# Edge counting in a graph transformer: the order in which ScalarE empties PSUM at the borders between target tiles

## The chip, the cores and the metric

The kernel runs on one core of a Trainium2 chip. The metric is the time of one execution on the device in microseconds (us), lower being better. Three timed runs of the kernel before gave 2011.37, 2013.77 and 2014.79 us; the median is 2013.77 us. One more execution was recorded by the hardware profiler, and every row below is of that one.

## What is computed

Two layers of a graph transformer on 1250 nodes with 768 features and 20000 edges (`src`, `dst`, sorted by `dst`). In each layer a graph branch and a linear-attention branch are added to the residual stream, and a mixture of eight experts follows. The graph branch of the first layer is a graph attention with 12 heads of width 64; cut to what matters here:

```python
def gnn0(h, src, dst, W, attn_l, attn_r, W_res):
    ft = einsum('nhd,od->nho', h.reshape(n, 12, 64), W)
    a1 = sum(ft * attn_l, -1)
    a2 = sum(ft * attn_r, -1)
    e = leaky_relu(a1[src] + a2[dst], 0.2)
    w = exp(e - segment_max(e, dst)[dst])
    alpha = w / segment_sum(w, dst)[dst]
    agg = segment_sum(alpha[:, :, None] * ft[src], dst)
    return relu(agg + res)
```

The weight of an edge depends on its pair (src, dst) alone. So the kernel first counts how many edges each pair of nodes has, as a dense 1250 x 1250 matrix, and every sum over edges becomes a matmul with that matrix. The second layer's graph convolutions use the same counts.

## The kernel before

The nodes are cut into NT = 10 tiles of T = 125. The stage concerned is the **edge counting**, which lies between the projection of the first layer's linear attention and the attention over the graph; in the profile it spans some 374 to 537 us.

**The counts of one target tile.** For target tile g, VectorE walks over the tiles of 125 edges that can hold an edge to it, six slots (SLOTS) to a turn. For each edge tile it writes two one-hot matrices: OHD (125 edges x 125 targets, L1677) and OHS (125 edges x 1250 sources, L1679; three of its slots are called OHA and three OHB in the profile). TensorE multiplies them (L795) in three pieces of 418, 416 and 416 columns (CH) into three PSUM banks: banks 0 to 2 for even g, 3 to 5 for odd g. How many turns a target tile takes is read from the data (`table`, L788 on TensorE, L1666 on VectorE). In this input, target tile 0 takes 54 edge tiles, tile 1 takes 24, tiles 2, 3 and 4 take 18 each and tiles 5 to 9 take 12 each. VectorE may run six edge tiles ahead of TensorE (`oh_free`). A last tiny matmul of zeros (L806) signals `acc_done`.

**From counts to the matrix AT.** ScalarE copies the three banks into AROW (L1220, one of two buffers by g % 2): rows are targets, columns are sources. The attention wants it transposed. So TensorE turns the ten 125 x 125 blocks of AROW in three rounds `("at", g, q)` of 4, 4 and 2 transposes (L781), and ScalarE copies each round from PSUM into AT (L1205).

**Rounds for the features.** Two more rounds for each g, `("ft", g, 0)` and `("ft", g, 1)`, multiply the normalised features by the weights W (L775). ScalarE empties such a round with six copies into F, scaled by row factors (L1201).

**Two banks for all rounds.** All rounds share PSUM banks 6 and 7 in turn. The list TRR fixes one order for them, and TensorE, before it fills round r, waits until round r - 2 is emptied (`tr_emptied`, in `turn_round`). The order is

```python
    for g in range(NT + 1):
        if g < NT:
            TRR += [("ft", g, 0), ("ft", g, 1)]
        if g:
            TRR += [("at", g - 1, q) for q in range(3)]
```

**The order at a border.** For each g, TensorE issues the two ft rounds of g, then counts g, then signals `acc_done`, then issues the three at rounds of g - 1 (whose rows lie in AROW since the border before). The at rounds of the last tile follow behind the loop. ScalarE, written out by hand in the same way, empties the two ft rounds of g, waits for `acc_done` of g, copies the three pieces of the rows of g (L1220) and then empties the three at rounds of g - 1 (`empty_round`, L1193 to L1206). The rows of g are needed by TensorE only at the next border (`arow_ready`, L779), and their banks only when it begins to count g + 2 (L802). ScalarE works through its instructions in order; so does TensorE. No DMA and no GpSimd instruction takes part in a border. SyncE waits once for the last round (L513) before it loads the third block of rows for the attention.

Of the kernel before, what the change touches and what calls it, by code (L numbers as in the profile page):

```python
# [15 lines left out]
NT, T = 10, 125  # L16
# [124 lines left out]
def graph_transformer(nc, xn_d, y_d, x, src, dst, gW, gWT, gWresT, attnT, w0, wp0, bp0, rwT, rb, ewT, eb,  # L141
# [988 lines left out]
    def _(act):  # L1130
# [62 lines left out]
        def empty_round(r):  # L1193

            kind, g, q = TRR[r]
            act.wait_ge(tr_filled, r + 1)
            ps = PS[0:T, 6 + r % 2, :]
            if kind == "ft":
                for k in range(6):
                    h = 6 * q + k  # L1200
                    nc.scalar.activation(F[:, g, h, 0:D], ps[:, k * D:(k + 1) * D], ACT.Copy, scale=P2[:, g, h:h + 1])  # L1201
                nc.scalar.drain().then_inc(tr_emptied, 1)
            else:
                w = min(4 * q + 4, NT) - 4 * q
                nc.scalar.activation(AT[:, 4 * q:4 * q + w, g * T:(g + 1) * T],  # L1205
                                     ps[:, 0:w * T].rearrange("p (s n) -> p s n", s=w), ACT.Copy).then_inc(tr_emptied, 1)  # L1206

        round_of = {key: r for r, key in enumerate(TRR)}
# [4 lines left out]
        for g in range(NT):  # L1213
            for q in range(2):
                empty_round(round_of["ft", g, q])
            act.wait_ge(acc_done, g + 1)
            if g >= 2:
                act.wait_ge(tr_filled, round_of["at", g - 2, 2] + 1)
            for c, (o, n) in enumerate(CH):
                nc.scalar.activation(AROW[:, g % 2, o:o + n], PS[0:T, 3 * (g % 2) + c, 0:n], ACT.Copy).then_inc(arow_ready, 1)  # L1220
            if g >= 1:
                for q in range(3):
                    empty_round(round_of["at", g - 1, q])
        for q in range(3):
# [131 lines left out]
        for r in range(18):  # L1356
            q, c = r // 3, r % 3
# [22 lines left out]
        for r in range(18):  # L1380
            q, c = r // 3, r % 3
# [650 lines left out]
```

## Time and profile before

| | |
|---|---|
| median of three timed runs | 2013.77 us (2011.37 to 2014.79) |
| the profiled execution, its own time | 2016.99 us |
| its span (first to last instruction) | 2015.1 us |
| TensorE matmuls, busy | 1849.3 us, 92% of the span |
| VectorE busy | 746.1 us, 37% |
| ScalarE busy | 401.5 us, 20% |
| mean granted TensorE clock | 0.957 of full |

In the profile PE is TensorE's matmuls, PEld its loads of stationary operands, DVE VectorE, ACT ScalarE, POOL GpSimd, SP SyncE; L1220 is line 1220 of the kernel. Matmuls are pipelined, so their busy times overlap a little. "issue" in the chain of waits is time in which an engine waited for nothing that the profile shows. PEclk is the granted clock of TensorE as a share of full speed; the two levels are 2.4 GHz (1.00) and 1.2 GHz (0.50), and a stretch that holds both shows a value between.

### The profile page before, as it was taken

Reading aid. Unit: us, or ns where it says so; the run is one execution under the profiler, and the core shown is the slowest. Engines: PE = TensorE matmul, PEld = TensorE weight load, DVE = VectorE, ACT = ScalarE, POOL = GpSimd, SP = SyncE. Lnnn points to the kernel's source line nnn. Section 1 sums busy time; section 2 is a strip of 40 time slices with the busy share of each in tenths; the row PEclk is TensorE's granted clock in tenths of the full one; section 3 lists DMA queues with packets and bytes.
Section 4 is the critical chain, followed back from the end, with each engine's and each line's share of the span. In section 5 each row is a group of like instructions: output and inputs, shape, how many; then the busy total and the mean of one; then the engine's idle time right before and its main releaser. Section 6 shows DMA issues by size and latency. Waiting matters only on the chain.

```text
span 2015.1 us, 24539 instructions
## 1 busy us (share of the span) xinstructions
PE 1849.3 (92%) x8418; PEld 1165.9 (58%) x8419; DVE 746.1 (37%) x1688; ACT 401.5 (20%) x1065; POOL 128.5 (6%) x212
## 2 busy tenths in 40 slices
PE   7999999998899998599997999999999999599980
PEld 4555566566533344366666965555588589365650
DVE  3212222686688989511114311141111133311114
ACT  2431210024211222111102422000221211222110
POOL 0000000000000000111114100000000000111105
PEclk9999999999899999699998999999999999699995
DMA  6004000000000101545556111010010011545437
GB/s 183 0 1 165 3 1 0 20 1 1 14 35 33 44 28 42 196 142 185 190 185 169 55 47 47 0 47 0 1 47 1 0 55 47 203 141 182 177 117 229
DMA packets 58060, 153.06 MB, mean 76 GB/s; under 512 B 12526, under 2 KB 23170, under 8 KB 57525
## 3 DMA queue, kind: packets, MB, share of 16 engines
q1 hardware_dynamic: 34053, 87.05, 12.5%
q0 software_dynamic: 13120, 35.86, 5.9%
q10 hardware_dynamic: 10800, 28.98, 3.9%
q8 instruction: 56, 0.92, 0.2%
q14 instruction: 31, 0.25, 0.0%
HBM read 121.37 MB, written 33.99 MB: 77 GB/s over the span
## 4 chain that ended last, share of the span: by engine, by line
PE 81%; DVE 8%; DMA 5%; issue 2%; DVEq 2%; ACT 1%; POOL 1%; ACTq 0%; SPq 0%; POOLq 0%
PE PS L646 23%; PE PS L975 10%; PE PS L656 7%; PE PS L795 6%; PE PS L1016 4%; PE PS L1085 4%; PE PS L717 4%; PE PS L1105 4%; PE PS L1057 4%; DVE WRA L1727 3%; PE PS L1043 3%; PE PS L884 2%; DMA WS<-in_fW 2%; PE PS L893 2%; DVE WRB L1727 2%
## 5 line engine op out<-in xcount | busy, mean ns | idle before, releaser
L646 PE MATMUL PS<-WS,XT 128*125 128x384 f32 x960 | 313.3, 488 | 1.4 <-issue 1.4
L646 PEld LDWEIGHTS PS<-WS,XT 128*125 128x125 f32 x960 | 180.4, 189 | 129.3 <-issue 3.4
L975 PE MATMUL PS<-WS,XGT 128*128 x600 | 199.9, 491 | 0.0
L975 PEld LDWEIGHTS PS<-WS,XGT 128*128 128x128 f32 x600 | 113.2, 192 | 74.7 <-issue 2.5
L656 PE MATMUL PS<-XT,WS 128*128 128x416 f32 (+1 forms) x432 | 151.2, 512 | 0.0
L1727 DVE SCALAR_TENSOR_TENSOR WRA<-RB,U,AT 125x500 f32<-125x500 f32 (+1 forms) x240 | 140.1, 648 | 9.5 <-ACT AT L1205 6.8
L1856 DVE TENSOR_TENSOR YS<-PS,EBB 128x768 f32<-128x768 f32 x48 | 46.0, 958 | 256.9 <-PE PS L975 192.1
L656 PEld LDWEIGHTS PS<-XT,WS 128*128 128x128 f32 x432 | 81.6, 189 | 69.2 <-issue 69.2
L884 PE MATMUL PS<-WRA,F 125*64 125x500 f32 (+1 forms) x480 | 100.5, 537 | 10.1 <-DVE WRA L1727 9.5
L1085 PE MATMUL PS<-WS,XGT 128*128 x288 | 101.9, 505 | 7.6 <-DMA WS<-in_fW 4.9
L1105 PE MATMUL PS<-WS,HT 128*128 x276 | 94.5, 493 | 2.5 <-ACT HT L1414 2.5
L582 POOL DMA_INDIRECT XG<-xn_rows,IDX x52 | 50.9, 979 | 680.9 <-DVEq L1821 643.6
L1297 ACT ACTIVATE XGT<-PS 128x384 f32<-128x384 f32 x102 | 44.4, 489 | 223.0 <-DVE YS L1856 184.7
L1085 PEld LDWEIGHTS PS<-WS,XGT 128*128 128x128 f32 x288 | 54.9, 197 | 43.3 <-issue 13.4
L1016 PE MATMUL PS<-XT,WS 128*128 128x250 f32 x360 | 79.1, 381 | 0.6 <-issue 0.6
L646 PE MATMUL PS<-WS,QT 128*125 128x384 f32 x240 | 78.9, 486 | 0.0
L646 PE MATMUL PS<-WS,QK 128*125 128x384 f32 x240 | 77.6, 486 | 0.0
L1105 PEld LDWEIGHTS PS<-WS,HT 128*128 128x128 f32 x276 | 53.2, 193 | 39.8 <-issue 4.2
L717 PE MATMUL PS<-XT,WS 128*128 128x416 f32 (+1 forms) x216 | 76.1, 513 | 0.0
L1374 ACT ACTIVATE HF<-PS,DT 125x384 f32<-125x384 f32 x40 | 23.2, 580 | 262.8 <-PE PS L646 262.8
L1057 PE MATMUL PS<-HH,AT 125*125 125x384 f32 x400 | 73.8, 344 | 1.9 <-DVE HH L1939 1.9
L1016 PEld LDWEIGHTS PS<-XT,WS 128*128 128x128 f32 x360 | 69.3, 194 | 9.3 <-issue 1.0
(293 smaller groups left out, 2244.6 us busy)
## 6 DMA issues: line engine op xcount, KB each, us to landing
WS<-in_ewT SPq DMA_DIRECT2D x8, 2304.0 KB, 10.6
expert_rows<-YS ACTq DMA_DIRECT2D x48, 384.0 KB, 2.3
WS<-in_fW SPq DMA_DIRECT2D x16, 1152.0 KB, 7.5
WS<-in_w SPq DMA_DIRECT2D x5, 2304.0 KB, 10.4
xn_rows<-XN ACTq DMA_DIRECT2D x20, 336.0 KB
RB<-expert_rows SPq DMA_DIRECT2D x12, 488.3 KB
WS<-in_wp SPq DMA_DIRECT2D x2, 2304.0 KB, 11.5
WS<-in_W SPq DMA_DIRECT2D x2, 2304.0 KB, 8.1
```

The lines of the kernel that those rows point to most:

```text
L646: last = nc.tensor.matmul(ps[0:T, 0:HC], lhsT[:, k, t * T:(t + 1) * T], w[:, k, b * HC:(b + 1) * HC], start=(k == 0), stop=(k == KC - 1))
L656: last = nc.tensor.matmul(ps[:, 0:n], w[:, k, q * P:(q + 1) * P], rhs[:, k, o:o + n], start=(k == 0), stop=(k == KC - 1))
L717: last = nc.tensor.matmul(ps[:, 0:n], w[:, k, q * P:(q + 1) * P], XT[:, k, o:o + n], start=(k == 0), stop=(k == KC - 1))
L795: last = nc.tensor.matmul(PS[0:T, 3 * (g % 2) + c, 0:w], OHD[:, k, :], OHS[k][:, o:o + w], start=(first and k == 0), stop=True, skip_group ...
L884: last = nc.tensor.matmul(num[j * D:(j + 1) * D], F[:, s, 2 * p + j, 0:D], WR[k % WSLOTS][:, j, 0:n], start=(s == 0), stop=(s == NT - 1), ...
L975: last = nc.tensor.matmul(PS[:, 4 + 2 * a + b, 0:HC], XGT[:, a, k, :], WS[:, bass.ds(slot, 1), k * C + b * HC:k * C + (b + 1) * HC].rearra ...
L1016: last = nc.tensor.matmul(ps[:, 0:n], w[:, k, q * P:(q + 1) * P], XT[:, k, o:o + n], start=(k == 0), stop=(k == KC - 1))
L1043: last = nc.tensor.matmul(ps[:, 0:n], HH[:, v, s, q * P:(q + 1) * P], AT[:, s, o:o + n], start=(s + v == 0), stop=(s == NT - 1 and v == 1))
L1057: last = nc.tensor.matmul(ps[0:T, 0:HC], AT[:, s, t * T:(t + 1) * T], HH[:, v, s, b * HC:(b + 1) * HC], start=(s + v == 0), stop=(s == NT ...
L1085: last = nc.tensor.matmul(PS[:, 2 + a, 0:FH], XGT[:, a, k, :], WS[:, bass.ds(slot, 1), k * FH:(k + 1) * FH].rearrange("p a b -> p (a b)"), ...
L1105: last = nc.tensor.matmul(PS[:, 5 + b, 0:HC], HT[:, k, :], WS[:, bass.ds(slot, 1), o:o + HC].rearrange("p a b -> p (a b)"), start=(k == 0) ...
L1727: V.scalar_tensor_tensor(out=WR[k % WSLOTS][:, j, 0:nt * T], in0=RBS[u % RSLOTS][:, j, 0:nt * T], scalar=U[:, s, h:h + 1], in1=AT[:, s, t0 ...
```

## The change

For g from 1 to 8, ScalarE empties the three at rounds of tile g - 1 before it waits for `acc_done` of g and copies the rows of g. For g = 9 the order stays as it was, and for g = 0 there are no at rounds. TensorE's, VectorE's and all other instructions are the same, and ScalarE issues the same instructions as before, in another order.

```diff
         for g in range(NT):
             for q in range(2):
                 empty_round(round_of["ft", g, q])
+            if 1 <= g < NT - 1:
+                for q in range(3):
+                    empty_round(round_of["at", g - 1, q])
             act.wait_ge(acc_done, g + 1)
             if g >= 2:
                 act.wait_ge(tr_filled, round_of["at", g - 2, 2] + 1)
             for c, (o, n) in enumerate(CH):
                 nc.scalar.activation(AROW[:, g % 2, o:o + n], PS[0:T, 3 * (g % 2) + c, 0:n], ACT.Copy).then_inc(arow_ready, 1)
-            if g >= 1:
+            if g == NT - 1:
                 for q in range(3):
                     empty_round(round_of["at", g - 1, q])
         for q in range(3):
             empty_round(round_of["at", NT - 1, q])
```

## Rows read from the trace of the kernel before

**Rows 1.** The page: busy time of TensorE; its granted clock in 40 slices.

```profile
PE 1849.3 (92%) x8418; PEld 1165.9 (58%) x8419; DVE 746.1 (37%) x1688; ACT 401.5 (20%) x1065; POOL 128.5 (6%) x212
...
PEclk9999999999899999699998999999999999699995
```

**Rows 2.** Chain of waits, 374 to 545 us: by line; the border at 441 us (start, length).

```profile
by line: PE PS L795 64.9%; PE PS L775 12.1%; ACT AROW L1220 7.0%; ACT AT L1205 5.0%; issue 3.9%; PE PS L884 3.6%; PE PS L781 3.3%; DVE WRA L1727 0.8%; PE PS L806 0.3%
...
440.99 0.05 PE PS L806
...
441.06 1.34 ACT AROW L1220 x3
442.40 0.49 ACT AT L1205
...
442.94 0.49 PE PS L781 x2
443.45 0.39 ACT AT L1205
...
444.26 2.13 PE PS L775 x12
446.39 10.73 PE PS L795 x54
```

**Rows 3.** Waits, 374 to 545 us (total us, times, longest).

```profile
PE PS L781 <- ACT AT L1205: 8.9, 10, 1.0
PE PS L775 <- ACT AT L1205: 6.6, 8, 0.8
...
DVE OHD L1677 <- PE PS L795: 34.3, 20, 3.8
```

**Rows 4.** Chain of waits, the last border, at 533 us.

```profile
534.66 1.19 PE PS L781 x6
...
535.88 0.60 ACT AT L1205
...
536.51 0.49 PE PS L781 x2
```

**Rows 5.** TensorE's timeline (start, length; idle before): transposes at 441, two pauses elsewhere.

```profile
440.86 1.11 PE L781 MATMUL PS<-ident,AROW 125*125 125x125 f32 x8
...
1479.38 3.87 PE L1043 MATMUL PS<-AT,HH 125*128 125x418 f32 x19 [1.91 <-ACT HH L1376]
...
1628.99 4.26 PE L1057 MATMUL PS<-HH,AT 125*125 125x384 f32 x14 [1.87 <-DVE HH L1939]
```

**Rows 6.** Chain of waits: the border at 410 us, which has no transposes.

```profile
409.77 0.79 issue
410.56 1.57 PE PS L775 x12
```

**Rows 7.** Chain of waits: behind the border at 457 us.

```profile
460.36 1.57 PE PS L775 x12
461.93 9.63 PE PS L795 x54
```

**Rows 8.** Windows (start:end length, busy time of each engine, PEclk, DMA share, GB/s).

```profile
444.20:448.00 3.80, 3.73 (x18) 3.16 (x19) 0.46 (x3) 2.67 (x12) 0.00 (x0) 0.62 0.00 0
...
460.30:464.00 3.70, 3.64 (x25) 3.14 (x26) 1.60 (x6) 2.58 (x12) 0.00 (x0) 1.00 0.00 0
...
1479.40:1483.00 3.60, 3.60 (x19) 3.55 (x20) 0.00 (x0) 0.00 (x0) 0.00 (x0) 1.00 1.01 393
...
1629.00:1632.50 3.50, 3.50 (x12) 3.50 (x13) 0.00 (x0) 0.00 (x0) 0.00 (x0) 0.58 1.02 376
```

**Rows 9.** VectorE's timeline: the first six one-hot pairs of target tile 6.

```profile
495.36 0.26 DVE L1677 TENSOR_SCALAR OHD<-iota,ES 125x125 bf16<-125x125 f16 x1 [1.51 <-PE PS L795]
...
498.60 0.55 DVE L1679 TENSOR_SCALAR OHB<-iota,ES 125x1250 bf16<-125x1250 f16 x1
```

**Rows 10.** Chain of waits: TensorE's counting of target tile 6.

```profile
501.10 7.48 PE PS L795 x36
```

## The prediction, made before the changed kernel ran

> **What bounds the kernel now.** The page comes first: TensorE is busy for 92% of the span, so little can be won but where it waits, or where its clock is below full [rows 1]. The clock row says that full speed is not held throughout, which matters below. Then the chain of waits over the counting stage. Most of it is TensorE's: counting (L795), the feature rounds (L775), the transposes (L781). But 7.0% are ScalarE's row copies (L1220) and 5.0% its copies into AT (L1205) [rows 2]. They are on the chain at each border with transposes, and the border at 441 us shows how. Counting ends at 440.99; ScalarE copies the three pieces of rows for 1.34 us; only then does it empty the first transposed round (0.49), which sets free the bank for TensorE's last two transposes at 442.94. The copy of the second round shares that stretch, the third follows (0.39), and the next feature rounds begin at 444.26. The rows just copied are wanted by nobody until the next border.
>
> The waits give the total: TensorE waits 8.9 us in ten waits for the copies into AT before transposes, and 6.6 us in eight before feature rounds. VectorE waits 34.3 us for TensorE, so it isn't the bound here [rows 3].
>
> **The change, part by part.**
>
> *Row copies off the chain.* The change concerns eight borders (g = 1 to 8). ScalarE issues the same 3 + 3 copies; nothing is added or removed, on no queue. The 3 row copies (1.34 us) leave the path at each, but not all of that is won, because the first transposed round must be filled before it can be emptied. TensorE starts the first eight transposes at 440.86 [rows 5]. What follows if ScalarE stands ready is seen in the last border, where the rounds of tile 9 meet an idle ScalarE: six transposes take 1.19, of which the first two take 0.49 as in rows 2, so four take 0.70. Then 0.03 until the copy, 0.60 for the copy (0.49 when another stands just before it), 0.04 until the next transposes: 0.70 + 0.03 + 0.60 + 0.04 = 1.37 us from the first transpose of a round to the round that reuses its bank [rows 4]. At 441 us the same distance is 442.94 - 440.86 = 2.08 [rows 2, 5]. **Gain 0.71 us a border, 8 x 0.71 = 5.7 us.** Bounds: 0 if the next wait takes it all, 1.34 x 8 = 10.7 if the fill cost nothing. I take the measured distance.
>
> *Do the feature rounds follow?* They start 444.26 - 442.94 = 1.32 after the last two transposes. Two things lie in it: ScalarE's third copy, and TensorE's own reading of the table for the next tile. The border at 410 us has no transposes at all, and there TensorE still pauses 0.79 us, all "issue" [rows 6]. Behind the last transposes (442.94 + 0.49 = 443.43) the pause is 0.83, nearly the same. So the table reading sets it, it starts behind the transposes, and moves with them. The copies: first emptied at 440.86 + 1.33 = 442.19, second 442.68, third fill at 442.23 + 0.49, emptied by 443.14. The feature rounds at 442.94 - 0.71 + 1.32 = 443.55 wait for neither.
>
> *The row copies in their new place.* They run from 443.14 to 444.48. Behind them on ScalarE queue the feature copies (L1201), whose first round is only filled some 0.9 us behind 443.55; so they lose nothing, and nobody needs them before the next border. Cost zero, under cover of TensorE's feature rounds and counting (over 7 us at the shortest). The next tile counts into the banks of tile g - 1, copied a border earlier.
>
> *VectorE as the next one late.* Behind a border TensorE needs edge tiles. Six were made in 495.36 to 499.15, 3.79 us, or 0.63 each [rows 9]; TensorE takes 9.63 / 18 = 0.535 each at full clock [rows 7]. VectorE is slower by the piece, but the border gives it time: here its sixth piece is ready at 499.15, and TensorE begins to count at 501.10 [rows 10]. With both savings of this border (0.71, and 0.60 that half clock adds to the feature rounds there) it would begin near 499.8 and reach the sixth 5 x 0.535 = 2.7 us later. Cost zero. For target tile 0 VectorE does set the pace, but that is before the change acts.
>
> *The clock.* Behind the border at 441 us the granted clock is 0.62, behind the one at 457 it is 1.00 [rows 8]. Feature rounds and 18 edge tiles take 2.13 + 10.73 = 12.86 us in the first case and 1.57 + 9.63 = 11.20 in the second [rows 2, 7]: a fall to 1.2 GHz costs 1.66 us. In the windows and the chain, five of the eight borders concerned show such a fall (428, 444, 475, 499, 523 us), three don't (460, 488, 512), although the pauses are alike. In each TensorE idles in two parts: between the first eight transposes and the last two (442.94 less 440.86 + 1.11, or 0.97 [rows 2, 5]) and ahead of the feature rounds (0.83), 1.8 us; the change takes 0.71 of the first and leaves 1.1 us. What did the clock do elsewhere? Behind 1.91 idle us at 1479 it stayed at 1.00, behind 1.87 at 1629 it fell [rows 5, 8]; behind 0.79 at 410 it stayed, since the feature rounds took 1.57 as at full clock [rows 6, 7]. So 1.8 us is where it can go either way, and 1.1 us lies towards the shorter pause, where it held. **Gain: 5 x 1.66 = 8.3 us if all falls go.** Bounds: 0, or a loss of 3 x 1.66 = 5.0 if all eight borders fall.
>
> The Trainium skill ("TensorE: Matmul & The Clock Gate", "A second HAM failure mode: psum-queue depth-cycling") holds that many brief idle moments between groups of matmuls suffice for the clock to swing up and down. By that rule the falls would stay, and this term would be 0 instead of 8.3 us. The trace bears it out only as far as the pauses of 1.8 us go.
>
> *Sum.* 5.7 + 8.3 = 14.0 us from the profiled execution's own 2016.99 gives 2003.0. That execution's span is 2015.1, with 1.9 around it, and its time lies 3.2 us over the median. If the 3.2 is what profiling adds, the median becomes 1999.8. If it is that the timed runs had two falls fewer (2 x 1.66 = 3.3), they have fewer to win, and the median becomes 2003. I can't tell which, and take **2002**.
>
> **The rivals.**
>
> *The falls stay.* If pauses of 1.1 us serve the fall as well as 1.8, only 5.7 us are won: 2008.1 on the median, 2011.3 on the profiled time. For it speaks that the fall is not governed by the idle time alone (like pauses, unlike outcomes). Against it: the 410 us border, and the attention stage behind this one, which is full of small waits, with the clock near full in its slices [rows 1]. With some falls left it lies between 2002 and 2008.
>
> *No gain: the next wait takes it.* The feature rounds stay where they are because they wait for something that doesn't move. Against it: each candidate (third copy, table reading, VectorE) starts from an event that does move. The change does what it says, since the wait for `acc_done` is what stands ahead of the copies now. Time: 2013.8.
>
> *Slower: more falls.* TensorE's clock falls at each of the eight borders and again in the counting behind it, 16 stretches in place of 5: 11 x 1.66 = 18.3 lost, 5.7 won, 12.6 us slower, 2026. It decides from 11 falls on the counting stage: (11 - 5) x 1.66 = 10.0 less 5.7 is 4.3 us slower. For it: the moment of a fall depends on more than the pause. Against it: no border shows two falls, and the change takes idle time away and puts none in.
>
> **How the numbers follow.** Falls gone 0.66 (2002); falls stay in part or whole 0.21 (2005 to 2011); no gain 0.10; slower 0.03. A measurement of this kernel tells 0.2%, about 4 us, from no change. Faster by more than that: all of the first, most of the second (5.7 us is just over the bound): 0.84. Within it: 0.13. Slower: 0.03. Range: 1998 (both gains off the median, and near 2 us that three runs scatter) to 2009 (only the first gain, on the median).
>
> **What would show it.** In the changed kernel's profile: at eight borders the copy into AT starts some 0.7 us behind the first transposes, the last two transposes 1.37 behind it, and the row copies stand behind the third AT copy; the wait of TensorE's transposes for ScalarE falls from 8.9 to about 3 us, that of the feature rounds stays near 0.8 each under whatever name. Counting behind 18-tile borders takes 9.63 each time, with PEclk at 1.00 in all. The last border is unchanged. The stages from 537 us on have their old lengths, but start some 14 us sooner. Wrong it would be if feature rounds still began 3.3 us behind the end of counting, if PEclk below 1.00 stood behind borders with shorter pauses, or if a later stage grew by as much.

## The result, and the profile after

The changed kernel takes 1999.29 us (median of four runs, 1998.45 to 1999.94) against 2012.57 us before (four runs, 2009.52 to 2014.79). The ratio is 0.9931 with an interval of 0.9919 to 0.9944, which is 11 to 16 us less. The forecast was 2002, with 1998 to 2009 as its range.

The profiled execution (1999.16 us, span 1997.3) shows the borders in another form. First the chain of waits in the changed kernel from 374 to 545 us: its shares by line, then the border at 440 us (start, length, what), to be held against [rows 2].

```profile
by line: PE PS L795 62.6%; PE PS L775 9.6%; PE PS L884 8.2%; PE PS L781 5.9%; ACT AT L1205 5.5%; issue 3.8%; PE PS L893 2.7%; DVE WRA L1730 0.8%; ACT AROW L1223 0.8%; DVEq L1667 0.5%; PE PS L806 0.1%
...
440.02 0.01 PE PS L806
440.03 0.55 PE PS L781 x4
440.58 0.02 issue
440.60 0.60 ACT AT L1205
441.20 0.04 issue
441.24 0.49 PE PS L781 x2
441.74 0.02 issue
441.76 0.39 ACT AT L1205
442.15 0.42 issue
442.57 1.57 PE PS L775 x12
444.14 9.63 PE PS L795 x54
```

The row copies (now L1223) fell from 7.0% of the chain to 0.8%, which is the last border, left as it was. In their place stand the first four transposes and the first copy into AT. From the end of counting to the feature rounds it was 444.26 - 440.99 = 3.27 us, and is 442.57 - 440.02 = 2.55. Over the eight borders these stretches sum to 26.0 us before and 20.2 after: **5.8 us from the order**. The feature rounds with the counting behind them take 1.57 + 9.63 here, where the same border had 2.13 + 10.73.

ScalarE's timeline of the changed kernel at the same border shows where the row copies went (start, length, instruction, idle before).

```profile
440.60 1.54 ACT L1205 ACTIVATE AT<-PS 125x500 fp32r<-125x500 f32 x3 [8.06 <-PE PS L781]
442.04 1.33 ACT L1223 ACTIVATE AROW<-PS 125x418 f32<-125x418 f32 x3
443.52 2.77 ACT L1201 ACTIVATE F<-PS,P 125x64 f32<-125x64 f32 x12
```

Three AT copies, three row copies, and the feature copies start 0.95 us behind the feature rounds' own start at 442.57, as early as they could before: the row copies are fully covered.

Windows on the changed kernel, from each of two of the eight feature rounds on (start:end length, busy time of each engine, PEclk, DMA share, GB/s); the other six read 1.00 too.

```profile
442.50:446.20 3.70, 3.63 (x25) 3.13 (x26) 2.15 (x8) 3.45 (x15) 0.00 (x0) 1.00 0.00 0
...
501.50:505.00 3.50, 3.47 (x24) 3.02 (x25) 2.02 (x7) 3.29 (x15) 0.00 (x0) 1.00 0.00 0
```

**All five falls of the clock are gone**: 1.57 + 4 x 1.66 = 8.2 us. The waits of the changed kernel from 374 to 545 us (total, times, longest):

```profile
DVE OHD L1680 <- PE PS L795: 21.2, 17, 1.6
...
PE PS L775 <- ACT AT L1205: 6.5, 8, 0.8
...
PE PS L781 <- ACT AT L1205: 3.1, 10, 1.0
```

Against [rows 3], TensorE's wait ahead of transposes fell from 8.9 to 3.1 us, that ahead of the feature rounds stayed (6.6 to 6.5), and VectorE waits 21.2 us in place of 34.3. The whole stage, from the feature rounds of tile 0 to the first attention weight of VectorE, went from 163.33 to 149.05 us, 14.3 less: 5.8 from the order, 8.2 from the clock at these borders, and 0.3 from the counting of target tile 0 (35.64 to 35.37 us with its feature rounds), which the change does not touch.

The two profiled spans differ by 17.8 us. The stage began 1.6 us later in the changed kernel and gave 14.3. The other 5.1 us are 0.9 between the stage and the first gather of tokens, 1.5 from there to the last store of expert rows, and 2.7 behind it. No instruction differs there. From the end of the stage to the end of the span it was 1477.7 and 1474.3 us in two profiles of the kernel before (the second is below) and 1472.5 and 1476.2 in two of the changed kernel. The two ranges overlap, so these 5 us are scatter between executions and are not credited to the change. Of the 0.9 us, 0.8 can be located: the first 16 matmuls of the attention (L884), at half clock in their first part, took 6.10 us before and 5.27 in the changed kernel.

### The profile page after: what moved, and what is told of

Same layout as the page of the kernel before. It is cut to its first block, busy times and chain, and to the rows that moved or that the text cites. A ratio compares the mean times of both kernels' runs of the same rounds, so it can differ in the third digit from the quotient of the medians.

```text
span 1997.3 us, 24539 instructions
## 1 busy us (share of the span) xinstructions
PE 1838.2 (92%) x8418; PEld 1157.3 (58%) x8419; DVE 745.1 (37%) x1688; ACT 401.4 (20%) x1065; POOL 128.5 (6%) x212
## 4 chain that ended last, share of the span: by engine, by line
PE 81%; DVE 8%; DMA 5%; issue 2%; DVEq 2%; ACT 1%; POOL 1%; ACTq 0%; SPq 0%; POOLq 0%
PE PS L646 23%; PE PS L975 10%; PE PS L656 8%; PE PS L795 5%; PE PS L1016 4%; PE PS L1085 4%; PE PS L717 4%; PE PS L1105 4%; PE PS L1057 4%; DVE WRA L1730 4%; PE PS L1043 3%; PE PS L884 2%; DMA WS<-in_fW 2%; PE PS L893 2%; DVE WRB L1730 2%
## 5 line engine op out<-in xcount | busy, mean ns | idle before, releaser
L884 PE MATMUL PS<-WRA,F 125*64 125x500 f32 (+1 forms) x480 | 100.1, 535 | 10.1 <-DVE WRA L1730 9.5
```

The lines of the kernel that those rows point to most:

```text
L884: last = nc.tensor.matmul(num[j * D:(j + 1) * D], F[:, s, 2 * p + j, 0:D], WR[k % WSLOTS][:, j, 0:n], start=(s == 0), stop=(s == NT - 1), ...
```

## The experiments

Two numbers describe the borders of a kernel. **Idle** is TensorE's idle time there: its waits for ScalarE ahead of the transposes (less the 1.2 us of the last border) and ahead of the feature rounds, over eight. **Falls** are the borders of g = 1 to 8 whose feature rounds and counting take 1.6 to 1.7 us longer than at full clock. The stage is measured as above, in the profiled execution; idle, falls and stage are thus of one execution each. A ratio compares a kernel with runs of the kernel before on the same chip, so kernels are compared with each other by their ratios rather than by their medians.

| kernel | idle, us | falls | stage, us | time, us | ratio to before (interval) |
|---|---|---|---|---|---|
| before | 1.8 | 5 | 163.3 | 2012.57 | |
| before, again | 1.8 | 4 | 161.5 | 2012.87 (one run) | |
| changed | 1.05 | 0 | 149.1 | 1999.29 | 0.9931 (0.9919 to 0.9944) |
| changed, again | 1.1 | 0 | 149.2 | 2000.23 | 0.9926 (0.9912 to 0.9940) |
| old order, idle time filled | 0.8 | 0 | 155.0 | 2004.46 | 0.9951 (0.9938 to 0.9965) |
| new order, two copies ahead | 1.9 | 5 | 164.4 | 2016.71 | 1.0013 (1.0004 to 1.0022) |
| new order, one copy ahead | 1.5 | 2 | 156.2 | 2007.03 | 0.9967 (0.9956 to 0.9979) |
| first round only | 1.45 | 0 | 152.4 | 2004.18 | 0.9954 (0.9940 to 0.9967) |
| borders 1 to 4 only | 1.05 / 1.8 | 1 | 153.9 | 2005.47 | 0.9967 (0.9955 to 0.9980) |
| new order at all nine borders | 1.05 | 0 | 150.2 | 2002.4 | 0.9949 (0.9932 to 0.9967) |
| old order, table read early | 0.95 | 0 | 147.9 | 1999.14 | 0.9926 (0.9910 to 0.9942) |
| new order, table read early | 0.25 | 0 | 142.1 | 1993.33 | 0.9900 (0.9885 to 0.9915) |

**The kernel before, again.** No edit.

> The kernel before, profiled once more, to see how many of its borders fall to half clock in another execution. Theory A (a fall costs 1.66 us and sits behind borders with 1.8 us of idle time): counting stage 374 to 537 us again near 163 us, 2 to 6 of the eight borders with a feature round and count stretch 1.66 us longer, the others at full clock. Theory B (the falls of the first trace were an accident of that execution): none or one, and the stage near 155 us.

Four borders fell (429, 474, 498 and 511 us), the other four did not, and the stage took 161.5 us. So falls are a trait of the kernel before, at changing borders, and not of one execution.

**The clock alone: the idle time filled in the old order.** The fillers write into banks that the next tile's counting clears anyway.

```diff
                 for q in range(3):
+                    if q == 2 and g < NT - 1:
+                        for _ in range(2):
+                            nc.tensor.matmul(PS[0:T, 3 * ((g + 1) % 2), 0:2 * P], XT[:, 0, 0:T], WBD, start=True, stop=True)
                     turn_round(round_of["at", g - 1, q])
```

> The old order of ScalarE, with two matmuls of 256 columns whose result nobody reads put into TensorE's idle 0.97 us ahead of the last two transposes of borders 1 to 8. It isolates the clock. Theory A (the clock falls because TensorE idles there): distances at a border unchanged (2.08 us to the last transposes, 3.3 us to the feature rounds), no falls, 5 x 1.66 = 8 us faster, near 2004. Theory B (falls don't depend on this pause): 2 to 6 falls stay, 2012 as before. Theory C (the fillers delay the transposes): up to 8 x 0.5 = 4 us of the gain is eaten.

TensorE's timeline of this kernel at one border:

```profile
439.63 1.12 PE L781 MATMUL PS<-ident,AROW 125*125 125x125 f32 x8
440.59 1.03 PE L812 MATMUL PS<-WBD,XT 128*125 128x256 f32 x4
441.71 0.48 PE L781 MATMUL PS<-ident,AROW 125*125 125x125 f32 x2
443.00 1.57 PE L775 MATMUL PS<-WBD,XT 128*125 128x128 f32 x12 [0.81 <-ACT AT L1208]
```

The last two transposes start 2.08 us behind the first, as before. Over the eight borders the stretches from the end of counting to the feature rounds sum to 26.1 us against 26.0, so nothing was won by order. Yet no border falls, the stage is 8.3 us shorter, and the ratio says 7 to 12 us. Work that nobody reads makes the kernel faster because TensorE keeps its clock. Theory A holds.

**The pause put back in the new order.** In the changed kernel, ahead of the first AT copy:

```diff
             if 1 <= g < NT - 1:
+                act.wait_ge(tr_filled, round_of["at", g - 1, 0] + 1)
+                for i in range(2):
+                    nc.scalar.activation(AROW[:, g % 2, 416 * i:416 * i + 416], X[:, g, 0:416], ACT.Copy)
                 for q in range(3):
                     empty_round(round_of["at", g - 1, q])
+                nc.scalar.drain()
```

> The new order, with two copies of 416 columns from SBUF to AROW (which the row copies overwrite later) ahead of the first AT copy at borders 1 to 8: the pause is put back without the row copies. Distance from first transposes to the last two goes from 1.36 to about 2.2 us. Theory A: the order term comes back as 8 x 0.85 = 6.8 us and the falls come back too, 4 to 5 x 1.66 = 7 to 8 us, so 2013 to 2014, as the kernel before. If the clock does not depend on the pause but on something else that the new order changed: 6.8 us only, near 2006.

TensorE's timeline at a border that fell:

```profile
426.12 1.11 PE L781 MATMUL PS<-ident,AROW 125*125 125x125 f32 x8
428.36 0.48 PE L781 MATMUL PS<-ident,AROW 125*125 125x125 f32 x2 [1.12 <-ACT AT L1205]
429.66 1.91 PE L775 MATMUL PS<-WBD,XT 128*125 128x128 f32 x12 [0.82 <-ACT AT L1205]
```

The distance is 2.24 us, the stage 164.4, five borders fall, and the time is as before, even 0.1% over it. The new order alone is worth nothing where the pause stays. That it is a little slower fits the pause, 0.16 us longer at each border than in the kernel before.

**Half the pause.** The same with one copy (`range(1)`).

> The new order with one copy of 416 columns instead of two ahead of the first AT copy: TensorE idles some 1.1 + 0.5 = 1.6 us a border. The order term of 8 x 0.5 = 4 us comes back. Falls between none (as with 1.45 us where only the first round was moved) and 4 or 5 (as with 1.8 us): 2003.5 if none, 2011 if five.

TensorE idles 0.68 us ahead of the last two transposes and 0.82 ahead of the feature rounds. Two borders fell in the profile and the stage took 156.2 us. The median of 2007.03 lies between the two cases; 12 runs spread from 1999.01 to 2010.44, the widest of all kernels here.

**Only the first round in the new order.** Against the changed kernel:

```diff
             if 1 <= g < NT - 1:
-                for q in range(3):
+                for q in range(1):
                     empty_round(round_of["at", g - 1, q])
...
-            if g == NT - 1:
-                for q in range(3):
+            if g >= 1:
+                for q in range(0 if g == NT - 1 else 1, 3):
                     empty_round(round_of["at", g - 1, q])
```

> New order for the first transposed round alone at borders 1 to 8: ScalarE empties round 0, then copies the rows, then empties rounds 1 and 2. The last two transposes start as early as in the changed kernel (1.36 us). Theory A: now the feature rounds wait for round 1 to be emptied, 0.55 + 0.02 + 0.60 + 1.34 + 0.49 + 0.04 = 3.0 us behind the end of counting, against 3.27 before and 2.54 in the changed kernel: 8 x 0.23 = 1.8 us from the order; TensorE idles some 1.45 us a border, so falls may stay or go (0 to 5 x 1.66): 2002.5 to 2011. Rival (only the table reading behind the transposes sets the feature rounds): they start at 2.54, all falls gone, 1999 as the changed kernel.

TensorE's timeline at a border:

```profile
440.51 1.11 PE L781 MATMUL PS<-ident,AROW 125*125 125x125 f32 x8
441.86 0.48 PE L781 MATMUL PS<-ident,AROW 125*125 125x125 f32 x2 [0.24 <-ACT AT L1205]
443.57 1.58 PE L775 MATMUL PS<-WBD,XT 128*125 128x128 f32 x12 [1.23 <-ACT AT L1205]
```

The last two transposes start 1.35 us behind the first, but the feature rounds wait 1.23 us, for the copy of round 1 behind the row copies. From the end of counting they start at 443.57 - 440.64 = 2.93 us (3.0 expected, 2.54 by the rival). Here a ScalarE copy sets them; in the changed kernel it does not. No border falls. That also tells something on the length of single pauses: the longest here, 1.23 us, is longer than any at a border of the kernel before (0.97), where about half of the borders fell. So the longest single pause does not decide, and the sum of the pauses (1.45 us here, 1.8 there) puts these kernels in the right order.

**Four borders.** The conditions of the change read `1 <= g < 5` and `g >= 5`.

> The new order at borders 1 to 4 alone; 5 to 8 as before. Theory A (each border stands by itself): 4 x 0.72 = 2.9 us from the order, no falls at borders 1 to 4, two or three at 5 to 8, so 2.9 + 2.5 x 1.66 = 7 us of the changed kernel's 14: near 2006.5. Rival (falls move to the borders that keep their pause, all four of them fall): 2.9 + 1 x 1.66 = 4.6 us, near 2009.

Borders 1 to 4 pass without a fall. Of borders 5 to 8, which keep the long pause, one fell (503 us). So the falls don't gather on the borders that keep their pause, and 2005.47 is close to the 2006.5 of theory A; on the same chip the changed kernel took 2000.23.

**The last border too.** The new order at g = 9 as well.

> The new order at the last border too (g = 9), which the change leaves out. There the rows are needed at once by the rounds of tile 9. In the changed kernel 520.04 to 524.75 = 4.7 us pass from the end of counting to the last AT copy; with the new order 2.1 us for the rounds of tile 8, then 1.34 for the rows, then 0.70 + 0.03 + 0.60 + 0.04 + 0.49 + 0.02 + 0.39 = 2.3: 5.7 us, so 1.0 us slower than the changed kernel, 2000.3. Rival (the new order is as good there): 1999 or less.

The chain of waits of this kernel at the last border:

```profile
519.60 0.01 PE PS L806
519.61 0.55 PE PS L781 x4
...
521.62 1.34 ACT AROW L1223 x3
522.96 0.14 issue
523.10 0.68 PE PS L781 x4
...
524.96 0.39 ACT AT L1205
```

From the end of counting to the last copy it is 525.35 - 519.60 = 5.75 us against 4.71 in the changed kernel. Here the fresh rows are what is waited for, and the old order is right. The stage is 1.1 us longer. The 3 us between the medians (2002.4 and 1999.29) are not evidence: the two kernels were not timed side by side, and the intervals of their ratios overlap.

**The table read early.** TensorE reads its two table entries for g + 1 behind the first turn of counting g.

```diff
+        def entries(g):
+            return (nc.tensor.value_load(table[0:1, 1, g:g + 1], min_val=2, max_val=TURNS),
+                    nc.tensor.value_load(table[0:1, 2, g:g + 1], min_val=0, max_val=TURNS * NT))
+
+        ahead = entries(0)
         for g in range(NT):
-            n = nc.tensor.value_load(table[0:1, 1, g:g + 1], min_val=2, max_val=TURNS)
-            done_before = nc.tensor.value_load(table[0:1, 2, g:g + 1], min_val=0, max_val=TURNS * NT)
+            n, done_before = ahead
...
             counted(done_before, True)
+            if g + 1 < NT:
+                ahead = entries(g + 1)
```

> The new order, and TensorE reads the table entries of tile g + 1 behind the first turn of counting tile g instead of at the border. Theory A (the table reading is what sets the feature rounds, and it moves): the pause ahead of the feature rounds goes from 0.83 us to next to nothing, and they start when round 1 is emptied, 0.55 + 0.02 + 0.60 + 0.49 + 0.04 = 1.70 us behind the end of counting instead of 2.54: 8 x 0.84 = 6.7 us, and 0.79 at the border behind tile 0, 7.5 in all; near 1992. Rival (the third AT copy sets them): 2.11 + 0.04 = 2.15, 3 us only, near 1996. Rival (reading stalls TensorE's queue in the counting instead): 1999, as the changed kernel.

The chain of waits of this kernel, one border:

```profile
438.69 0.01 PE PS L812
438.70 0.55 PE PS L781 x4
439.25 0.02 issue
439.27 0.60 ACT AT L1211
439.87 0.04 issue
```

TensorE's timeline behind it:

```profile
439.91 0.48 PE L781 MATMUL PS<-ident,AROW 125*125 125x125 f32 x2 [0.24 <-ACT AT L1211]
440.39 0.81 PE L775 MATMUL PS<-WBD,XT 128*125 128x128 f32 x5
```

The feature rounds follow the last transposes at once, 440.39 - 438.70 = 1.7 us behind the end of counting, as theory A had it. The stage loses 6.9 us against the changed kernel. Of the 7.5 expected, 0.4 went to VectorE at target tile 1: TensorE now arrives sooner there, feature rounds with 24 edge tiles take 1.41 + 13.38 us in place of 1.57 + 12.84, and from 411 to 425 us VectorE is busy for 14.00 of 14.00 us (13.74 in the changed kernel). At **1993.33 us (ratio 0.9900, 0.9885 to 0.9915) this is the fastest kernel of the study**, ahead of both. The same early reading in the old order of ScalarE:

> The old order of ScalarE, and only the early reading of the table. Theory A: the last two transposes still start 2.08 us behind the first, the feature rounds follow when round 1 is emptied, 0.07 + 1.34 + 0.49 + 0.49 + 0.04 = 2.4 to 2.6 us behind the end of counting in place of 3.27: 8 x 0.7 = 5.6 us and 0.8 at the first border. TensorE's idle time per border drops to about 1.0 us, so the falls go too (5 x 1.66 = 8.3): near 1999, as the changed kernel. If only ScalarE's order matters for the falls: 6.4 us, near 2007.

The feature rounds start 2.43 us behind the end of counting, no border falls, and 1999.14 us equals the changed kernel (ratios 0.9926 and 0.9931) without touching ScalarE. It is another way to the same shorter pause.

**The changed kernel, again.** No edit.

> The changed kernel once more, beside the kernel before on another chip. Theory A (the executions of the kernel before scatter because the number of falls at its borders differs, and the changed kernel has none): near 1999.3, its runs within some 2 to 3 us of each other, those of the kernel before over some 8 us. If the falls are only moved or rarer: its runs scatter as widely as those of the kernel before.

The time came out (2000.23), the scatter did not: five runs from 1994.92 to 2002.22, while ten of the kernel before lay between 2010.78 and 2015.02. Its profile has no fall and a stage of 149.2 us. So the falls at these borders are not the main source of scatter between executions. TensorE's clock in other stages is a candidate. In these five runs the mean granted clock was 0.966, 0.965, 0.963, 0.962 and 0.962 for 1994.92, 1996.82, 2000.23, 2000.84 and 2002.22 us, and the 12 runs with half the pause go from 0.966 for the fastest to 0.959 to 0.960 for the four slowest. One place is in the traces: the first 16 matmuls of the attention took 5.27 us in one profile of the changed kernel and 6.46 in the other, against 3.50 for 16 of them at full clock. How much of the scatter that makes up stays open.

## Why the prediction was right

- **Row copies off the chain.** Forecast 8 x 0.71 = 5.7 us, measured 5.8. The 1.37 us taken from the last border came out as 1.35, since a fill and a copy by an idle ScalarE are the same pieces there.
- **The feature rounds follow.** Forecast 1.32 us behind the last transposes, as before; measured 442.57 - 441.24 = 1.33. The early reading of the table shows by experiment that TensorE's own reading filled that pause: moved away, the feature rounds start where the transposes end.
- **The row copies in their new place.** Forecast zero, measured zero at these borders. The first-round-only kernel shows what they cost where the cover is missing: over the eight borders 23.4 us from counting to feature rounds against 20.2, or 0.4 us a border.
- **VectorE.** Forecast zero, and still true in the changed kernel. It first costs something (0.4 us in all) where another 0.8 us a border is taken away.
- **The clock.** Forecast 8.3 us if all falls go, measured 8.2 against the profiled execution with its five falls. The filled kernel shows the cause (idle time, not order), the two paused ones show the falls back. The prediction gave this 0.66 and had one short pause (0.79 us at 410) to go by; that the two parts of a pause may be added was assumed there, and the first-round-only kernel bears it out. What the runs do not tell apart is idle time and the length of the whole stretch from counting to feature rounds, transposes included: both shrink together (3.4 us with five falls, 3.2 before, 3.0 with two, 2.9 and less with none) in all kernels but the filled one, where 1.03 us of the 3.2 were matmuls. The Trainium skill ("TensorE: Matmul & The Clock Gate", "A second HAM failure mode: psum-queue depth-cycling"), weighed in the prediction, would have left the falls in place. The trace does not agree for pauses this short: with 1.05 to 1.1 us of idle time at each border, in two parts, none of 16 borders in two profiles fell.
- **The sum against the median.** This was the one weak step. Forecast 2002 stood between 1999.8 and 2003, because the profiled execution lay 3.2 us over the median and that was taken for either profiling or two more falls. Profiling does not add it: the changed kernel's profiled execution sits on its median (1999.16 and 1999.29). Two more falls are not borne out either, as far as two profiles go: the kernel before fell four times in an execution of 2012.87 us and five times in one of 2016.99, so one fall explains 1.7 of these 4.1 us, and the rest is scatter in other stages. How often the timed executions fell is not recorded. With five falls the gains off the median give 2013.77 - 14.0 = 1999.8, with four 2001.4; both lie within 2.2 us of the 1999.29 measured, which the scatter between runs does not resolve.
- **The rivals.** Falls that stay: out, in the profiles of all kernels with at most 1.45 us of idle time. A next wait that takes it all: out. More falls and a slower kernel: out.

## What to carry to other kernels

At a border between stages an in-order engine should first do what another engine is waiting for, and only then what is wanted a whole stage later; where the later work is itself waited for, as the rows at the last border here, the same swap costs time. A short pause of TensorE can cost more than its own length if its clock falls behind it: count the stretches at half clock before judging what a pause is worth, and consider filling it. When one wait has been shortened, look at the next piece in the same pause; here reading two table entries ahead was worth as much as the change's order term.

## What the runs showed of the hardware

- At these borders a fall of TensorE's clock has the same price each time: 1.66 us in nearly every case (1.57 once), whether 18 or 12 edge tiles follow. Elsewhere it varies: the first 16 matmuls of the attention (L884) took 5.27 to 6.46 us in the nine profiles that have all 16 on the chain, where 16 of them take 3.50 at full clock, so 1.8 to 3.0 us more.
- Like pauses have unlike outcomes. With 1.8 us of idle time in two parts, five borders of eight fell in one execution, four, partly others, in the next, and one of four in the kernel with the change at four borders. With 1.9 us five of eight fell. With 1.5 us in one kernel two fell, with 1.45 in another none, and with 1.1 or less none in five kernels. At the other end stands the way from the last border into the attention: TensorE idles some 3.2 us or more there in several parts (0.96 + 0.21 + 1.99 in the changed kernel), and in all twelve profiles the granted clock behind it was 0.55 to 0.67. The change leaves that fall where it was.
- Each of TensorE's two table entries took 0.30 us to load and 0.15 us to convert at the border, 0.8 us of pause for the pair (the first load starts 0.3 us before the last matmul). Placed inside the counting, where matmuls are queued, they cost TensorE nothing that the trace shows.
